# A graph network kernel: new sort of the edges, node work moved ahead of it and into its readback

## What is computed

```python
x_aug = jnp.concatenate([x, type_emb[node_types]], axis=-1)
attn = attn * rel_scale[edge_rel] / np.sqrt(DH)
inp['Wc1'], inp['bc1'] = lin(ks[10], 1, 32)
inp['Wc2'], inp['bc2'] = lin(ks[11], 32, HEADS)
inp['We'], inp['be'] = lin(ks[9], EDGE_DIM, HEADS)
inp['Wd1'], inp['bd1'] = lin(ks[12], 1, 16)
```

## Time and profile before

| | us |
|---|---|
| median of 3 runs | 7939.46 (7930.02 to 7971.64) |
| the profiled execution | 7918.95 |
| its span, first to last instruction | 7917.2 |

### The profile page before, as it was taken

One profiled execution on the slowest core, in us unless ns is written; L12 is line 12 of the kernel. 1 busy time (PEld: TensorE's weight loads), 2 busy tenths in 40 slices (PEclk: granted clock), 3 DMA queues, 4 the chain that ended last, 5 costly groups with the idle time before them and its releaser, 6 DMA issues. The chain is left out here.

```text
span 7917.2 us, 146985 instructions
## 1 busy us (share of the span) xinstructions
PE 5592.1 (71%) x31871; PEld 4510.9 (57%) x31872; DVE 5137.2 (65%) x18685; ACT 1400.5 (18%) x3612; POOL 5041.5 (64%) x4817
## 2 busy tenths in 40 slices
PE   2677777388888788887699899768888874555533
PEld 1666666266666566666455555447888753333322
DVE  7788888277777577777555555447777753555564
ACT  0333333022222121111122222100001110000000
POOL 0666666177777377777188888617777724777751
PEclk6555555699999899999799999977767775555556
DMA  1444444444444344445155555514545524333420
GB/s 64 110 110 111 110 109 106 148 131 131 131 130 130 74 130 132 132 130 128 28 83 80 80 80 83 88 39 128 131 129 130 132 39 76 85 85 86 85 58 26
DMA packets 929162, 791.02 MB, mean 100 GB/s; under 512 B 580951, under 2 KB 748308, under 8 KB 927668
## 3 DMA queue, kind: packets, MB, share of 16 engines
q0 software_dynamic: 264032, 434.24, 23.8%
q1 hardware_dynamic: 649788, 342.32, 17.7%
q10 hardware_dynamic: 15264, 13.50, 0.8%
HBM read 700.00 MB, written 88.28 MB: 100 GB/s over the span
## 5 line engine op out<-in xcount | busy, mean ns | idle before, releaser
L1005 POOL DMA_INDIRECT there<-table_wide,idx x1664 | 1584.6, 952 | 781.1 <-issue 550.0
L1588 POOL DMA_INDIRECT partial_sums<-row_sums1a,idx1a x632 | 1000.9, 1584 | 230.6 <-issue 184.8
L1912 POOL DMA_INDIRECT there<-table_wide,idx x832 | 828.8, 996 | 447.9 <-issue 248.6
L2353 POOL DMA_INDIRECT there<-table_narrow,idx x832 | 792.1, 952 | 485.0 <-issue 252.6
L649 POOL DMA_INDIRECT rec<-out_recd,posd x806 | 805.2, 999 | 396.6 <-issue 212.9
L1096 PE MATMUL ps<-here,hot_t 128*128 x3328 | 970.8, 416 | 82.7 <-DVE there L1047 62.5
L1104 PE MATMUL ps<-relu,hot_s 128*128 128x128 f32 x3328 | 759.0, 316 | 315.7 <-DVE hot_s L1036 312.3
L1521 PE MATMUL ps<-src_hot1a,edge_parts1a 128*128 128x512 bf16 x4800 | 868.4, 334 | 0.0
L2435 PE MATMUL ps<-here,hot_t 128*128 x1664 | 507.6, 463 | 494.6 <-DVE prod L2380 442.2
L1104 PEld LDWEIGHTS ps<-relu,hot_s 128*128 128x128 f32 x3328 | 560.6, 199 | 498.4 <-issue 470.9
L1047 DVE TENSOR_TENSOR there<-there,ps 128x512 f32<-128x512 f32 x832 | 567.5, 682 | 328.1 <-PE ps L1096 327.7
(11 more groups left out here) (413 smaller groups left out, 10338.9 us busy)
## 6 DMA issues: line engine op xcount, KB each, us to landing
locrows<-loc_row SPq DMA_DIRECT2D x416, 256.0 KB
krowd<-key_row SPq DMA_DIRECT2D x201, 256.0 KB
src_rows1a<-src_row SPq DMA_DIRECT2D x79, 512.0 KB
there<-table_wide,idx POOLq DMA_INDIRECT x2496, 2.8
lrowd<-lo_row SPq DMA_DIRECT2D x201, 128.0 KB
attr_raw<-in_edge_attr SPq DMA_DIRECT2D x201, 128.0 KB
there<-table_narrow,idx POOLq DMA_INDIRECT x832, 3.5
rec<-out_recd,posd POOLq DMA_INDIRECT x806
```

The costliest lines, as they stand in the source:

```text
L1005: nc.gpsimd.indirect_dma_start(there[:, j, q, :], None, table, bass.IndirectOffsetOnAxis(idx[:, j, q:q + 1], 0)).then_inc(gathered[j][q], 16)
L1588: nc.gpsimd.indirect_dma_start(sums[q % TABLES], bass.IndirectOffsetOnAxis(idx[:, j, q:q + 1], 0), out[:, j, q, :], None, compute_op=ALU.a ...
L1912: nc.gpsimd.indirect_dma_start(there[:, j, q, :], None, table, bass.IndirectOffsetOnAxis(idx[:, j, q:q + 1], 0)).then_inc(gathered[j][q], 16)
L2353: nc.gpsimd.indirect_dma_start(there[:, j, q, :], None, table, bass.IndirectOffsetOnAxis(idx[:, j, q:q + 1], 0)).then_inc(gathered[j][q], 16)
```

## The change

1. **The start.** Blanks, raw keys and x get buffers that live on (`Loads`). Its `begin` clears them on POOL and issues the loads of x, four weights and the keys. Then come turning of x (copied in pieces), layer norm, global vector and the first node rows; their table's store is not waited for. Then the key rows.
2. **Under the count.** `rest` issues the blanks, all other weights and the cleared sums; the sort's own weights follow, and the block's end waits for all.
3. **The placing loop.** Four record slots instead of two, four groups a turn. Within a group PE adds all counts at once into four columns of blocks in PSUM, ACT copies them with one instruction, PE does the four look-ups in a row; DVE picks with one product by the one-hot and one reduction. Distances and types lie as 16 rows for each of the 4 chunks, so a stack is 128 x 128 and takes three products for the four chunks, with the bias in the weights of the types; ACT moves the sums into the record.
4. **The readback.** While the records are read, `sorted_index` makes the type terms (stored in DRAM and read again under layer 2's norm), the gate of the nodes (kept) and, behind the index, the node ids. The three blocks in layers 2 and 3 go.
5. **Table stores** of `node_rows` go out in five parts.

```diff
-            fill_records(nc, rec)
-            load_keys(nc, k, a["src"], a["dst"], keys[:, :, 0], key_col, keys[:, :, 1], *key_rows, ps)
-            sort_edges(nc, k, key_col, keys[:, :, 1], keys, rec, g["block"], ps, key_rows, "d", a, (g["count"], g["begin"]))
-        sorted_index(nc, k, rec, g, ps)
-        w = load_weights(nc, top, a, k, sums)
-        load_nodes(nc, k, a["x"], xt, ps)
-        layer0(nc, k, w, g, table2, xt, ps)
+                loads.begin(nc)
+                layer0_start(nc, k, w, table2, rows, xt, ht, glob, ps, loads)
+                load_keys(nc, k, loads, keys[:, :, 0], key_col, keys[:, :, 1], *key_rows, ps)
+                sort_edges(nc, k, key_col, keys[:, :, 1], keys, rec, g["block"], ps, key_rows, "d", a, (g["count"], g["begin"]), loads)
+            sorted_index(nc, k, w, rec, g, a, ps)
+            layer0(nc, k, w, g, table2, xt, ht, glob, ps)
...
+            @block.sync
+            def _(sp):
+                loads.rest(sp, k)
+                terms.load_weights(sp)
+                loads.landed(sp)
...
+            SLOTS = 4
...
+    def load_rows(self, sp, i, h, whole=True):
+            for g in range(G):
+                sp.dma_start(row[first + g * HID_D:first + (g + 1) * HID_D, 2 * h:2 * h + 2, :],
+                             source[ds(at, 2 * G * P)].rearrange("(s g p) -> g s p", g=G, p=P)[g:g + 1].to_broadcast([HID_D, 2, P])).then_inc(arrived, 16)
...
-                        last = nc.vector.scalar_tensor_tensor(junk[:, j, g, P:P + NB], k["iota"][:, 0:NB], hi_col[:, ds(at + g, 1)], ps[:, 2 + (j * G + g) % 4, 0:NB],
-                                                              ALU.is_equal, ALU.mult, accum_out=base[:, j, g:g + 1])
+                    nc.vector.tensor_tensor(found[:, b, 0:n, 0:NB], ps[:, 2 + b, 0:n * NB].rearrange("p (g t) -> p g t", g=n), hot_hi[:, b, 0:n, :], ALU.mult).then_inc(chosen, 1)
+                    nc.vector.tensor_reduce(slot[:, b, 0:n], found[:, b, 0:n, :], AX.X, ALU.add).then_inc(summed, 1)
...
+                def count(b, g, first, last):
+                    return nc.tensor.matmul(ps[:, 0, first * NB:(last + 1) * NB].rearrange("p (r t) -> p r t", t=NB), hot_lo[:, b, g, :],
+                                            hot_hi[:, b, g, :][:, None, :].to_broadcast([P, last + 1 - first, NB]),
+                                            start=False, stop=True, skip_group_check=True)
...
+                for t in range(0, NB, STORED):
+                    sp.wait_ge(kept, t + STORED)
+                    sp.dma_start(dram[t * P:(t + STORED) * P, :].rearrange("(t p) f -> p t f", p=P), dest[:, t:t + STORED, 0:width]).then_inc(stored if later is None else later, 16)
```

More of the change, by code:

```diff
@@ L582, in _ @@
-                finish(PAIRS, 1, tail)
+                for j in range(SLOTS):
+                    ahead(*((0, j + 1) if j + 1 < SLOTS else (1, 0)), G)
+                    positions(0, j, G, False)
+                with dve.Fori(1, QUADS) as i:
+                    for j in range(SLOTS):
+                        ahead(*((i, j + 1) if j + 1 < SLOTS else (i + 1, 0)), G)
+                        positions(i, j, G, True)
+                ahead(QUADS, 1, tail)
+                positions(QUADS, 0, G, True)
@@ L616, in _ @@
+                terms.begin_tensor(pe)
+                terms.turn(pe, 0, 0)
+                with pe.Fori(0, QUADS) as i:
+                    for j in range(SLOTS):
+                        step(i, j, G, (i, j + 1) if j + 1 < SLOTS else (i + 1, 0))
+                step(QUADS, 0, G, (QUADS, 1, False))
+                step(QUADS, 1, tail, None)
             @block.scalar
             def _(act):
-                def step(i, j, n, before):
-                    at = i * (2 * G) + j * G
-                    for g in range(n):
-                        act.wait_ge(counted, at + (g + 2))
-                        nc.scalar.activation(run[:, j, g, :], ps[:, 0, 0:NB], ACT.Copy).then_inc(copied, 1)
-                    if before:
+                act.sem_inc(kept, 2)
@@ L641, in _ @@
+                with act.Fori(1, QUADS) as i:
+                    for j in range(SLOTS):
+                        step(i, j, G, (i, j + 1) if j + 1 < SLOTS else (i + 1, 0), True)
+                step(QUADS, 0, G, (QUADS, 1, False), True)
+                step(QUADS, 1, tail, None, True)
             @block.gpsimd
@@ L700, in _ @@
+            dve.wait_ge(split, 3)
+            for t in range(NT):
+                w_t = min(P, NV - t * P)
+                nc.vector.tensor_scalar(ids[0:w_t, t, :], ps[0:w_t, t, 0:P], first[0:w_t, t:t + 1], None, ALU.add).then_inc(made, 1)
         @block.tensor
         def _(pe):
+            pe.wait_ge(hotted, 1)
+            for at, to in SPANS:
+                nc.tensor.matmul(wide(ps)[:, at:to], w["type_emb"][:, :], kind_hot[:, at:to], start=True, stop=True).then_inc(tet_made, 1)
+            pe.wait_ge(vec_in, 16)
@@ L1176, in _ @@
         def _(pe):
+            pe.wait_ge(loads.first_in, 16 * len(loads.first))
             pe.wait_ge(scaled, 1)
```

828 lines of the change are left out of this document (406 added, 422 removed).

## The result

The changed kernel takes 7657.16 us (median of 4 runs, 7639.75 to 7683.1) against 7943.2 (4 runs, 7930.02 to 7971.64): a ratio of 0.9638, 95% interval 0.9598 to 0.9678. The forecast was 7670. The profiled execution took 7667.06 us, its span 7665.3; against the profiled one of before that is 251.9 us less, where the forecast's terms summed to 260. The medians lie 286 us apart, since the profiled run of before was 24 us under its median and that of after 10 us over its own.

A forecast was written before the change was run, and what follows sets the result against it. The prediction took POOL's scatter work as the sort loop's nearest floor. Its terms summed to −260 us from the profiled 7918.95, giving 7659, with 7670 us forecast because that run lay below the median; range 7590 to 7780.

The forecast's parts named there:

- The front: Work before counting starts, now including x, layer norm and first node rows: 70.7 us against 51.1, +19.6 us.
- Under the count: Blanks, weights and cleared sums, at most 93 us of DMA, hide under DVE's 137.6 us of counting: 0 us.
- E: Rival: work under the count is not covered, at worst +30 us; chance 0.03 together with C.
- The loop: Sort's placing loop: landing waits go, POOL sets 5.35 us a group instead of 5.82; −94 us, bounds −163 and 0.
- The readback: Reading records back: PE's gate chain outlasts the 29 us by 12, node ids add 1.9; +13.9 us, bounds 0 and +16.
- rival C: Readback cover is complete because PE is granted 2.4 GHz there: 7658 us; chance 0.03 together with E.
- −111.8: Between index and first gather, 1440.63 to 1552.42 us, no work is left: −111.8 us.
- Stores: Node table stores in five parts, three still waited for, last fifth at 3 us: −15.5 us, bounds −9 and −18.
- 8. and 9.: Layer 2 loses its type block, −23.3 us; layer 3 its ids block, −13.2, and its gate, −30.7.
- A: Rival: placing loop keeps its pace, 5.6 to 5.9 us a group, through PE's waits or late rows: 7764 us; chance 0.17.
- B: Rival: scatter hold-ups go, scatters at the minimum of 952 ns, loop 1041 us: 7633 us; chance 0.09.
- D: Rival: SP's 14 DMA issues for two groups bound the placing loop, +500 us on it, about 8260; chance 0.03.

The follow-up runs named there:

- three pairs of runs: Changed kernel and variants waiting for scatters of two groups ago instead of four, each pair on one chip: placing loop changed by +2.0, −2.5 and −7.5 us.
- turning the order: Changed kernel with all gate products behind the record transposes, then with 9 of 25 ahead: readback stage 49.0 and 46.3 us instead of 55.1.
- the edit: Changed kernel, gate last, with accumulation in the four rank comparisons replaced by one reduction: 0.9768 of the kernel before, against 0.9714 with accumulation.
- the three lots: Twelve follow-up kernels, run in three groups on three chips; the kernel before took 9970, 9934 and 9831 us there.

## Why the prediction held, point by point

1. The front: +22.0 for +19.6. The steps were right; what failed is the 2.9 us less for copying x in pieces. Loading, turning and copying x took 18.0 us (4.48 to 22.43) as before.
2. Under the count: 0.9 for 0. Right, E is refuted.
3. The sort's weights: −5.3 for −5. Right.
4. The loop. This term carried the error: −127.0 for −94, inside its bounds. The size came from POOL's floor plus "some 0.1 for the three waits and the admission", 5.35 us; the floor alone, 5.2, was right. So the step that failed in size is the 0.1 to 0.15 us a group. In mechanism another failed: "SLOTS = 4 lets ACT wait for scatters four groups old, so the 317 us go". They did not go, they grew to 573; and three pairs of runs give the ring nothing, beside a standstill that the profiles do not have. Which part of the change gave the 127 us is open: the ring, or the order of work, for which the estimate above speaks. By the trace of after, the rest of the loop's chain became shorter than POOL's, and POOL was rightly named as next. PE was foretold busy for over 85% and is at 74% (768.75 of 1044.30): 3.85 us a group where I had put 4.4 to 5.0. DVE at 3.6 was put at 4, which is near.
5. The readback: +15.5 for +13.9. Right in mechanism. DVE's first record copy starts 41.4 us after the stage's first instruction, where it started 29.1 after it before: +12.3 for 12. The cover itself was too short by only 9.6 us, for the records were issued 0.6 us into the stage and landed 30.9 later, not 29; what follows took 3.2 us more for 1.9. That is why turning the order gave 6.1 and 8.8 us and not 12. The granted clock was 0.53 in the stage, and 0.50 under the four products, so rival C is refuted.
6. −111.8: right, nothing was left of that stretch.
7. Stores: 3 us were foretold and the maximum is 3.4. By undoing it, 19.3 for 15.5.
8. and 9. The stretches ahead of layer 2's and layer 3's first gathers, stores included, got shorter by 30.4 us (from 5111.3 to 5307.5 before, 4936.4 to 5102.2 after) and 48.1 (6388.5 to 6591.9, 6175.6 to 6330.9). Foretold were 23.3 + 13.2 + 30.7 and the stores' share, some 10. Right. Layer 0's gathers took 2203.4 us for 2203.5, though a store of theirs got shorter; the loops of layers 2 and 3 and the tail moved by −7.6, +6.6 and +2.5, and layer 1 with its lead-in by +34.3.

The loop gave 33 us more than foretold and layer 1's stretch took 31 of them: the sum of the terms is right partly by luck, because these two cancel in the one profiled run. The medians, 286 apart, are nearer to what the terms give without that stretch, −252 − 31 = −283.

The rivals: A (the loop keeps its pace) is refuted by POOL's idle time. The chances do not fit the range: the forecast's own, A and B lie in 7590 to 7780 and add up to 0.94, while 2 in 10 are said to fall outside. B foretold scatters at 952 ns; they take 994, as the 999 before, so the hold-ups did not vanish. That the loop's 1044 us came so near to B's 1041 is luck: what was missing is the 0.1 to 0.15 us a group. The Trainium skill (SBUF — State Buffer, Who interferes with whom) names two kinds of DVE instruction that hold GpSimd up: one in a two-port mode, and one with two SBUF inputs against a GpSimd instruction that reads SBUF. No run here shows that or rules it out, since the edit removed none of either. D was not seen.

## What to carry to other kernels

A long wait at the end of a ring may say only that its owner is ahead: look at whether the engine that sets the pace waits, before the wait's microseconds are booked as gain. The floor of an engine that issues indirect DMAs is their count by busy time plus gap, and here, once every feeder was shorter, nothing came on top. A test of a wait belongs where the wait is: look first at whether the kernel before still has it there. Work put under a transfer has to be ordered so that what waits for the transfer does not stand behind it: ahead of the landing what fits, the rest behind it.

## What the runs showed of the hardware

- The same program took up to 26% longer in the three lots than in the first measurement (9637 against 7657 us for the changed kernel); that the chips differ is the obvious reason and is not shown. The readback is 55.1 us in both, and the scatters of the placing loop take 997 and 994 ns in the mean. Only loops are longer, and not all: layer 0's 1664 gathers took 3086 us for 2203 and the placing loop 1371 for 1044, but layer 1's scatters 1218 for 1250. In the placing loop the granted clock was 0.50 in both; in layer 0 it was 0.78 for 0.95, and PE's products were longer there (L1223: 502 ns for 417 in the mean), while the gathers took 959 ns for 954. Whether that is a cause or follows from a PE that waits more, and why the loops stand still, is open.
- A stretch of 632 scatters that POOL and DVE share varies by 40 us (1217.7 to 1257.1) between profiled runs of different kernels, and by 32 for one program, with the same minimum of 1542 ns for one. A difference of 0.5% in one profile can be that.
